# Native fp32 for the last two dense products of self-attention, with one copy of the sums and a new order of the last head group

## The reference

```python
def _L0_attn_ref(x, w_q, w_kv, w_dense):          # HEADS 16, GROUPS 4, KVC 128
    q = einsum('bsh,he->bse', x, w_q).reshape(b, sq, GROUPS, HPG, KVC)
    k, v = split(einsum('bsh,he->bse', x, w_kv), 2, axis=-1)
    scores = einsum('bqgpd,bkgd->bgqpk', q, k) * SCALE
    scores = where(causal, scores, -inf)
    probs = softmax(scores, axis=-1)
    ctx = einsum('bgqpk,bkgd->bqgpd', probs, v).reshape(b, sq, HEADS * KVC)
    return einsum('bse,eh->bsh', ctx, w_dense)
...
x = x + _L0_xattn_ref(_layernorm(x), ctx_1024, ...)
x = x + _L0_attn_ref(_layernorm(x), w_q, w_kv, w_dense)
x = x + _L0_ffn_ref(_layernorm(x), gate_w, ...)   # scores = sigmoid(x @ gate_w), top 2, experts
```

## Time and profile before

| | |
|---|---|
| median of three runs | 351.37 us |
| profiled execution | 349.24 us |
| its span, first to last instruction | 347.5 us |
| PE busy | 331.4 us (95%) |
| DVE, POOL, ACT busy | 271.0, 236.1, 232.4 us |
| chain of waits, PE's share | 71% |

### The profile page before, as it was taken

The page is one execution under the profiler, slowest core; times in us unless marked ns, Lnnn a source line. Parts: engine busy times, 40 slices in busy tenths (PEclk is TensorE's granted clock), DMA queues, the critical chain, the costliest instruction groups (busy, mean ns, idle before and its releaser), DMA issues.

```text
span 347.5 us, 6872 instructions
## 1 busy us (share of the span) xinstructions
PE 331.4 (95%) x2246; PEld 299.8 (86%) x2246; DVE 271.0 (78%) x469; ACT 232.4 (67%) x415; POOL 236.1 (68%) x146
## 2 busy tenths in 40 slices
PE   6899989999999999999999998999899999999995
PEld 5788868898999999999999987999798897698995
DVE  3787788897988988989889887754559745579997
ACT  3789467667687687777767775975355686266761
POOL 4593728798599599499598596859626768507650
PEclk9999999999999999999999999999999999999999
DMA  6811468776886895895795887890232040404630
GB/s 199 249 32 38 100 153 189 196 176 152 220 189 144 204 204 127 208 208 125 178 204 117 201 181 183 208 321 31 87 101 83 2 151 1 144 9 124 179 107 31
DMA packets 32566, 49.98 MB, mean 144 GB/s; under 512 B 5537, under 2 KB 23073, under 8 KB 32545
## 3 DMA queue, kind: packets, MB, share of 16 engines
q1 hardware_dynamic: 32544, 49.72, 56.6%
HBM read 20.08 MB, written 0.26 MB: 59 GB/s over the span
## 4 chain that ended last, share of the span: by engine, by line
PE 71%; DVE 9%; POOL 6%; issue 4%; ACT 4%; SPq 3%; DMA 2%; DVEq 0%; POOLq 0%; ACTq 0%
PE bank L573 10%; PE pair L573 10%; PE bank L574 10%; PE bank L575 10%; PE pair L574 10%; PE pair L575 10%; POOL pT L431 4%; SPq L272 3%; PE bank L717 2%; PE bank L876 1%; DMA ctx_raw<-in_ctx_dram 1%; DVE ctx_raw L1495 1%; PE bank L709 1%; PE pair L869 1%; DMA pT<-blocks 1%
## 5 line engine op out<-in xcount | busy, mean ns | idle before, releaser
L431 POOL TENSOR_TENSOR pT<-pT,pT_hi 128x1024 fp32r<-128x1024 f32 x56 | 133.4, 2407 | 35.3 <-ACT pT_hi L1135 35.3
L1125 ACT ACTIVATE probs<-probs,lowest 128x2048 f32<-128x2048 f32 x32 | 64.3, 2009 | 26.5 <-DVE lowest L1484 26.4
L1135 ACT ACTIVATE pT_hi<-pT 128x1024 fp32r<-128x1024 f32 x56 | 57.6, 1053 | 16.1 <-DMA pT<-ctx_raw 10.5
L573 PE MATMUL bank<-pT_hi,ctx_lo 128*128 128x256 f32 x224 | 63.8, 285 | 0.4 <-POOL pT L431 0.4
L574 PE MATMUL bank<-pT,ctx_hi 128*128 128x256 f32 x224 | 64.1, 286 | 0.0
L575 PE MATMUL bank<-pT_hi,ctx_hi 128*128 128x256 f32 x224 | 63.6, 284 | 0.0
L573 PE MATMUL pair<-ctxT_hi,qk_lo 128*128 128x512 f32 x128 | 52.1, 407 | 2.4 <-DVE lowest L1484 2.0
L575 PE MATMUL pair<-ctxT_hi,qk_hi 128*128 128x512 f32 x128 | 50.1, 391 | 0.0
L574 PE MATMUL pair<-ctxT_lo,qk_hi 128*128 128x512 f32 x128 | 50.1, 391 | 0.0
L1484 DVE CUSTOM_DVE_ANT_0 probs<-pair,mask_bias,lowest 128x1024 f32<-128x1024 f32 x32 | 41.0, 1281 | 9.3 <-PE pair L575 8.5
L431 POOL TENSOR_TENSOR ctx_lo<-ctx_raw,ctx_hi 128x512 fp32r<-128x512 f32 (+1 forms) x19 | 31.5, 1671 | 21.8 <-DVE route L1817 9.4
(11 more groups left out here) (253 smaller groups left out, 841.3 us busy)
## 6 DMA issues: line engine op xcount, KB each, us to landing
pT<-blocks SPq DMA_DIRECT2D x112, 128.0 KB, 2.3
pT<-ctx_raw SPq DMA_DIRECT2D x112, 128.0 KB, 2.3
ctx_raw<-ffn_experts_gate_up_dram SPq DMA_DIRECT2D x16, 256.0 KB, 2.8
wq<-in_L_xattn_Wq_dram SPq DMA_DIRECT2D x8, 256.0 KB, 2.6
ctx_raw<-in_ctx_dram SPq DMA_DIRECT2D x8, 256.0 KB, 6.4
wo<-in_L_xattn_Wo_dram SPq DMA_DIRECT2D x8, 256.0 KB, 2.8
blocks<-in_L_attn_w_dense_dram SPq DMA_DIRECT2D x4, 512.0 KB, 4.6
ctx_raw<-_L_ffn_experts_down_dram SPq DMA_DIRECT2D x16, 128.0 KB, 2.4
```

Of the source, the lines that this page charges most:

```text
L431: pool.tensor_tensor(dst, src, hi.bitcast(F32), ALU.subtract).then_inc(ready, 1)
L573: pe.matmul(dst, w[1], x[0], start=start, stop=False)
L1125: act.activation(probs[:, j], probs[:, j], ACT.Exp, bias=lowest[:, p, j, 1:2], scale=-1.0, accum_out=den[:, p, j:j + 1]).then_inc(exps, 1)
L1135: act.activation(hi_slot(c), chunk(p, c).bitcast(F32), ACT.Copy).then_inc(pT_hi_ready, 1)
```

## The change

- `dense_end` of the last two groups multiplies whole fp32 sums by whole fp32 weights in native matmuls, four for each group and batch, in place of twelve split ones. The sums have one copy each (`c2_whole`, in a buffer that the experts use later), with no rounding and no remainder.
- The rounding of these two groups' weights (DVE, ACT) and POOL's two subtractions are gone.
- The copy of group 2's sums is made by ACT for batch 0, ahead of its last exponentials, and by DVE for batch 1; both copies of group 3's are ACT's.
- DVE normalises the last group's probabilities in place of POOL.
- PE's order in the last group is new, and the eight `keep_warm` in it are gone; between the two transposes of the normed rows there is one `keep_warm` in place of two.
- ACT copies each batch's normed rows whole and then rounded; DVE subtracts from the whole copy in SBUF. PE waits for the remainders behind the logits, ahead of the first gate product.

```diff
@@ -178,6 +178,7 @@
         sg = ctx_raw[:, 3072:3584].rearrange("p (s t) -> p s t", s=2)
         hT = ctx_raw[:, 3584:4096].rearrange("p (s t) -> p s t", s=2)
+        c2_whole = ctx_raw[:, 3072:4096].rearrange("p (b n) -> p b n", b=B)
@@ -243,7 +244,8 @@
             sem("out_psum"), sem("added"))
         ld_wq2, ld_wkv2, ld_wd2 = [sem(f"ld_wq2_{i}") for i in range(2)], sem("ld_wkv2"), sem("ld_wd2")
-        ld_wd2_last, wd2_last_hi_ready = sem("ld_wd2_last"), sem("wd2_last_hi_ready")
+        ld_wd2_last = sem("ld_wd2_last")
+        c2_whole_ready = [sem(f"c2_whole_ready{b}") for b in range(B)]
         wq2_hi_ready, wk2_hi_ready, wd2_hi_ready = sem("wq2_hi_ready"), sem("wk2_hi_ready"), sem("wd2_hi_ready")
@@ -504,12 +506,8 @@
             def split_d(r):
-                if isinstance(r, int) and r == R - 1:
-                    pool.wait_ge(wd2_last_hi_ready, 1)
-                    rest(wq2_lo, wq2, wq2_hi, wd2_ready)
-                else:
-                    pool.wait_ge(wd2_hi_ready, r + 1)
-                    rest(wd2_lo, wd2, wd2_hi, wd2_ready)
+                pool.wait_ge(wd2_hi_ready, r + 1)
+                rest(wd2_lo, wd2, wd2_hi, wd2_ready)
@@ -541,9 +539,6 @@
             split_expert(0, 0)
             split_expert(0, 1)
-            split_d(R - 2)
-            split_d(R - 1)
-            normalise(R - 1)
             split_expert(0, 2)
@@ -890,14 +885,18 @@
             def dense_end(r, b):
-                hi, lo = (wq2_hi, wq2_lo) if r == R - 1 else (wd2_hi, wd2_lo)
-                pe.wait_ge(wd2_ready, r + 1)
-                pe.wait_ge(c2_ready, 2 * r + b + 1)
+                if r == R - 1:
+                    w = wq2
+                    pe.wait_ge(ld_wd2_last, 16)
+                else:
+                    w = wd2
+                    pe.wait_ge(ld_wd2, 16 * (R - 1))
+                    pe.wait_ge(added2, R - 2)
+                pe.wait_ge(c2_whole_ready[b], r - (R - 2) + 1)
                 for h in range(HR):
-                    cols = slice(h * P, (h + 1) * P)
-                    mm = product(D_LAST[b][:, b * H:(b + 1) * H], (c2_hi[:, b, cols], c2_lo[:, b, cols]),
-                                 (hi[:, h * H:(h + 1) * H], lo[:, h * H:(h + 1) * H]),
-                                 r == R - 2 and h == 0, r == R - 1 and h == HR - 1)
+                    mm = pe.matmul(D_LAST[b][:, b * H:(b + 1) * H], c2_whole[:, b, h * P:(h + 1) * P],
+                                   w[:, h * H:(h + 1) * H],
+                                   start=(r == R - 2 and h == 0), stop=(r == R - 1 and h == HR - 1))
                 if r == R - 1:
@@ -932,19 +931,16 @@
                 for b in range(B):
                     scores2(R - 1, b)
+                    attend2(R - 2, b)
+                dense_end(R - 2, 0)
+                turn2(R - 1, 0)
+                dense_end(R - 2, 1)
+                pe.wait_ge(v2_ready, R)
+                turn2(R - 1, 1)
                 for b in range(B):
-                    attend2(R - 2, b)
-                keep_warm(QB, 8)
-                turn2(R - 1, 0)
-                dense_end(R - 2, 0)
-                attend2(R - 1, 0)
-                turn2(R - 1, 1)
-                dense_end(R - 2, 1)
-                attend2(R - 1, 1)
+                    attend2(R - 1, b)
                 for b in range(B):
                     dense_end(R - 1, b)
-
-
@@ -989,10 +985,10 @@
-            for b in range(B):
-                xn_transpose(b, 2, (bank[2], bank[5])[b])
-                keep_warm(QA, 2)
-            pe.wait_ge(xnT_ready, 3 * B)
+            xn_transpose(0, 2, bank[2])
+            keep_warm(QA, 1)
+            xn_transpose(1, 2, bank[5])
+            keep_warm(QA, 2)
@@ -1028,6 +1024,7 @@
                                    start=(k == 0), stop=(k == HB - 1))
             mm.then_inc(logits, 1)
+            pe.wait_ge(xnT_ready, 3 * B)
             gate_up(0, 0)
@@ -1303,6 +1300,21 @@
                 act.activation(c2_hi[:, b], PC[b][:], ACT.Copy).then_inc(c2_hi_ready, 1)
+            def whole_c(r, b):
+
+                act.wait_ge(c2_psum, 2 * r + b + 1)
+                act.activation(c2_whole[:, b], PC[b][:], ACT.Copy).then_inc(c2_whole_ready[b], 1)
+
+            def last_group2():
+                whole_c(R - 2, 0)
+                for b in range(B):
+                    exps2(R - 1, b)
+                for b in range(B):
+                    act.wait_ge(p2T_psum, 2 * (R - 1) + b + 1)
+                    act.activation(p2T[:, b], TURN2_LAST[b][:], ACT.Copy).then_inc(p2T_ready, 1)
+                for b in range(B):
+                    whole_c(R - 1, b)
+
             def group2(r, before, behind):
@@ -1321,19 +1333,12 @@
                         act.wait_ge(ld_dn[s], 16)
                         act.activation(dn_hi[:, s], ring_dn[:, s], ACT.Copy).then_inc(dn_hi_ready, 1)
-
-                    act.wait_ge(qb_psum, R - 1)
-                    act.wait_ge(ld_wd2_last, 16)
-                    act.activation(wq2_hi, wq2, ACT.Copy).then_inc(wd2_last_hi_ready, 1)
                 if behind:
...
                     act.wait_ge(p2T_psum, 2 * r + b + 1)
-                    src = TURN2_LAST[b] if r == R - 1 else PC[b]
-                    act.activation(p2T[:, b], src[:], ACT.Copy).then_inc(p2T_ready, 1)
-                    if r == R - 1:
-                        copy_c(r, b)
+                    act.activation(p2T[:, b], PC[b][:], ACT.Copy).then_inc(p2T_ready, 1)
@@ -1354,7 +1359,7 @@
             for r in range(1, R - 1):
                 group2(r, True, True)
-            group2(R - 1, True, False)
+            last_group2()
@@ -1363,9 +1368,11 @@
                 act.activation(sg[:, s % 2], GU[s % 2][:, 0:B * T], ACT.Silu).then_inc(silu_ready, 1)
-            rows = [xnT_copy(b, 2, (bank[2], bank[5])[b]) for b in range(B)]
             for b in range(B):
-                xnT_copy_whole(b, 2, rows[b])
+                act.wait_ge(xnT_psum, 2 * B + b + 1)
+                rows = (bank[2], bank[5])[b][:, 0:HB * P].rearrange("p (k t) -> p k t", k=HB)
+                act.activation(xnT[:, :, b * T:(b + 1) * T], rows, ACT.Copy).then_inc(xnT_whole, 1)
+                act.activation(xnT_hi[:, :, b * T:(b + 1) * T], rows, ACT.Copy).then_inc(xnT_hi_ready, 1)
             act.wait_ge(logits, 1)
@@ -1719,7 +1726,7 @@
                 dve.tensor_tensor(rows, D_BANK[:], rows, ALU.add).then_inc(added2, 1)
-            def group2(r, before, behind, split):
+            def group2(r, before, split):
                 for b in range(0 if before else 1, B):
@@ -1730,22 +1737,38 @@
                 if split:
                     round_q(r + 2)
-                if before and behind:
+                if before:
                     add2(r - 1)
-                if behind:
-                    copy_qb(r + 1)
+                copy_qb(r + 1)
                 if split:
                     round_kv(r + 2)
-                if before and behind:
+                if before and split:
                     round_d(r)
+
+            def normalise_last(b):
+                dve.wait_ge(s2_rden, 2 * (R - 1) + b + 1)
+                dve.tensor_tensor(p2[:, b], p2[:, b], rd2[:, b].unsqueeze(2).broadcast_to([P, HR, P]),
+                                  ALU.mult).then_inc(s2_probs, 1)
+
+            def last_group2():
+                for b in range(B):
+                    scale2(R - 1, b)
+                    max2(R - 1, b)
+                invert(R - 1, 0)
+                normalise_last(0)
+                dve.wait_ge(c2_psum, 2 * (R - 1))
+                dve.tensor_copy(c2_whole[:, 1], PC[1][:]).then_inc(c2_whole_ready[1], 1)
+                copy_v(R - 1)
+                invert(R - 1, 1)
+                normalise_last(1)
             round_kv(1)
             first_qb(1, qb_psum, 1, qb_ready)
-            group2(0, False, True, True)
+            group2(0, False, True)
             for r in range(1, R - 2):
-                group2(r, True, True, True)
-            group2(R - 2, True, True, False)
-            group2(R - 1, True, False, False)
+                group2(r, True, True)
+            group2(R - 2, True, False)
+            last_group2()
@@ -1758,13 +1781,19 @@
                 norm_stats(b, 2)
-            rest_c(R - 1)
+            def xnT_rest_whole(b):
+                dve.wait_ge(xnT_whole, B + b + 1)
+                dve.wait_ge(xnT_hi_ready, 2 * B + b + 1)
+                cols = slice(b * T, (b + 1) * T)
+                dve.tensor_tensor(xnT_lo[:, :, cols], xnT[:, :, cols], xnT_hi[:, :, cols].bitcast(F32),
+                                  ALU.subtract).then_inc(xnT_ready, 1)
+
             finish_rows(0)
...
                 norm_apply(b, 2)
             for b in range(B):
-                xnT_rest(b, 2, (bank[2], bank[5])[b])
+                xnT_rest_whole(b)
```

## The result

In the same set of executions the kernel before took 351.15 us (median of 7, 349.68 to 351.54) and the changed one 348.79 (median of 7, 348.04 to 349.98); the ratio is 0.9939, 95% interval 0.9921 to 0.9957. A second set, with 12 and 29 executions, gave 349.09 against 350.21, ratio 0.9961 (0.9933 to 0.9988). The profiled execution of the changed kernel took 348.99 us, with a span of 347.1: only 0.25 less than the profiled execution before. The page shows one reason why this is so little: in one of the forty slices TensorE's granted clock was not full, while it was full throughout in the earlier trace rows.

The account below looks back on a forecast made before the run. Bound by a chain of PE alone up to about 289.5, then hand-overs among PE, ACT, DVE and POOL. Dense end 1.15 + entry 0.70 = 1.85 off 349.24 gives 347.39; plus 2.13 to the median, 349.5 us, range 348.8 to 350.6.

Parts of the forecast that it names:

- Dense calls (a): Last two groups' dense products: four native matmuls take 1.73 us a call against 1.43 split, adding 1.20 us of PE work.
- the rival with 1.90: Dense products: a native matmul costs four split ones, so 1.90 us a call, gain 1.15, end 350.2; chance 0.06.
- Order (b): PE's last head group: reordered steps without fillers end at 299.16 against 300.45, a gain of 1.29 us without waits.
- Waits (c): PE's hand-overs in the last group: 0.15 us charged for waits (none to 0.5), leaving 1.15 at the dense end.
- the 1.1 to 1.3 that the prediction had named as its sign: End of the dense products: DVE's last addition was to come 1.1 to 1.3 us earlier.
- Normalisation on DVE: Last group's probabilities: DVE normalises in 0.69 us, bounds 0.6 and 1.05, in place of POOL's 1.05.
- the rival that has it wait behind POOL: Last group: DVE's normalisation waits up to 1.27 us for a POOL piece, PE loses 1.1, end 350.6; chance 0.09.
- What goes away at no cost (d): Dropped roundings and POOL's subtractions cost nothing now; first down-projection reload moves from 297.88 to about 289, costed at nothing.
- The rival with a larger gain: Layer norm's stretch: reloads leave it and POOL is idle beside DVE, up to 0.7 us more, 348.8; chance 0.09.
- Entry (e): Feed-forward entry: whole rows copied first, so logits, exponential and router come 0.70 us earlier; gate products' wait costs 0.03.
- The rival that gives it back after the router: From 311.7, a fixed event at the expert splits sets the pace; 0.70 is lost, end 350.2; chance 0.12.
- its slower rival: After the dense end: TensorE's clock drops to 1.2 GHz, about 3.2 us more, end 352.7; chance 0.04.

Follow-up runs that it names:

- the run with the dense half alone: Kernel before plus the change's native dense products, new last-group order and DVE normalisation, with the old feed-forward entry; 349.59 us, ratio 0.9986.
- the undisturbed profile: Changed kernel, unaltered, profiled again, with no clock fall ahead of the gate products; end 59.87 us after the last head group's first scores (-1.67).

## Why the prediction was right, step by step

- **Dense calls (a).** Forecast 1.73, measured 1.73 (289.67 to 291.40, 296.15 to 297.88), as in the earlier trace rows, and the same in every run with native products where nothing held them. That is 1.21 times the 1.43 of the split form, and the rival with 1.90 fell. The Trainium skill, "FP8 and Floating Point Precision", section TensorE Precision Notes, has four passes for true fp32; the estimate of 1.91 drawn from it took a pass to be as long as a split matmul (0.119). The measured time doesn't speak against four passes, only against that: by them a pass would be 1.73/16 = 0.108 us, an estimate, as no row shows single passes.
- **Order (b).** Forecast 1.29 without waits. The new order has every step where it was put, and the run with the old order shows that this step carries the gain: 2.09 lie between the two (about 1.7 without ACT's share in it), against 1.20 that the slower products cost.
- **Waits (c): the term that was mis-sized.** Charged 0.15 with bounds of none to 0.5; measured 0.42: from the start of the first native product to the end of the last one PE took 297.88 + 1.89 - 289.67 = 10.10, where the prediction had 9.52 and a tail of 0.16. The second product waited 0.20 for DVE's copy, which began at 291.21 and ended at 291.89, and ran 0.07 longer for it (1.96 against 1.89). The four sums were stretched by 0.16, from 1.88 to 2.04: ACT's copy of the second turned block ended at 294.48 + 0.60 = 295.08, in time for a sum at 294.28 + 0.86 = 295.14, but PE's weight load stands behind the same wait, and that came only at 295.19. The row of weight loads (start, us, line, operation, shape, count, idle time before) shows it:

```profile
292.01 1.59 PEld L897 LDWEIGHTS pair<-blocks,ctx_raw 128*128 128x128 f32 x8 [0.24 <-issue]
...
295.19 0.30 PEld L871 LDWEIGHTS bank<-probs 128*128 128x128 f32 x2 [0.72 <-issue]
```

At both places the load starts 0.11 to 0.12 behind the end of the copy that it waits for; the prediction counted 0.03 for a hop, read from a POOL step to a turn and from ACT to DVE. The first cause was shown by taking the copy away from DVE (0.26); the second is read from the trace only. So the dense end gave 0.89 and not 1.15, and stayed under the 1.1 to 1.3 that the prediction had named as its sign.
- **Normalisation on DVE.** Forecast 0.69 between 0.6 and 1.05; measured 0.69. POOL was through with its splits at 287.55 + 2.51 = 290.06 and DVE began at 290.60, so the rival that has it wait behind POOL did not come up; its margin was 0.54.
- **What goes away at no cost (d).** The first reload of a down projection was issued at 289.00 (forecast about 289; the earlier trace rows has 297.88). From the addition to the exponential the kernel before takes 5.02, and the run with the dense half alone 5.01 though these reloads have left that stretch (DMA share 0.00 to 0.04 from 298 to 306): they cost nothing that a mark shows. The rival with a larger gain, which rested on them, fell with that.
- **Entry (e).** Forecast 0.70; measured 0.74 in the run that has this part alone, and 1.63 - 0.89 = 0.74 in the whole change. The rival that gives it back after the router fell: in the undisturbed profile the end has 1.67 of it all. At the silu, though, 0.19 to 0.20 of it is missing (-0.54 alone, -1.44 in the whole): there PE's gate products, which now wait for the remainders, decide and not the exponential, as the 0.20 of idle time ahead of the silu shows. The prediction had put this wait at 0.03. At the end it is back.
- **The sum.** Forecast -1.85, measured -1.67 from S to the end without a fall: 0.26 less at the dense end, 0.04 more at the entry.
- **The clock.** The prediction put its slower rival at 3.2 us, by the transposes, logits and first gate products together. A fall did come there, in one profile of the change out of two, later than thought and shorter: the transposes and logits were through at full clock, it began at about 304.1, and it cost 1.06. What the prediction held against it, no hole on PE before 299 and five fillers behind, did not prevent it. The place was right and the price three times too high. Executions with a mean granted clock of 0.995 or less are about as frequent before and after (55 of 78, 13 of 19), so the falls did not turn the sign.
- **Carrying the sum over to the median: in part luck.** The step "profiled execution plus 2.13" took the 2.13 for a fixed distance. It is made by the executions with a fall: the first profile of before had none. Profiles without a fall ahead of PE's last matmul took 349.24, 349.55 and 349.25 before and 347.96 after, 1.28 to 1.59 less. The measured 348.79 lies not in the forecast's own 349.1 to 350.0 but at the lower edge of the whole range, though the gain from S on was smaller than forecast. The medians differ by 351.15 - 348.79 = 2.36 because they stand for different levels: the 351.15 is near the 351.40 that executions of before with a mean clock of 0.99 or less have (the clocks of those seven are not known), and the middle one by clock of the seven changed ones has 0.995. One level is worth 351.40 - 350.24 = 1.16, which leaves 1.2 for the change. The second set gave 350.21 - 349.09 = 1.12. So the step gave a time within range, but was no reason. The 0.1 to 0.4 between the profiles' 1.28 to 1.59 and the 1.67 from S on lies mostly ahead of S, where PE's list is the same (S at 285.96, 286.30 and 286.00 before, 286.33 after without a fall); what moves it stayed open.

## What to carry to other kernels

A slower instruction can win where it takes steps out of a hand-over and lets the order fill the wait with work; price the order and the instruction separately, since here the one was worth 1.7 to 2.1 us and the other cost 1.20. When such an order leaves only tenths of cover, list each copy with its engine and the moment it is wanted: the copy charged at 0.1 was the longest wait, and another engine had room for it. Before a profiled difference is believed or carried over to a median, read the granted clock of both executions, compare marks on both sides of a fall, and compare executions of like mean clock.

## What the runs showed of the hardware

TensorE's granted clock fell to 1.2 GHz for 3 to 4 us in some executions of one and the same program and not in others. Where PE still had work it was seen at three places (53 to 58, 218 to 222 and 304 to 310 us), each behind a stretch with PE idle for part of the time; but PE was busy 2.02 of the 4 us from 50 to 54 in the profile of the kernel before that fell and 2.04 in the three that didn't, and the two profiles without fillers had the same gaps ahead of the gate products and differed all the same. What decides it was not found. Ahead of the gate products a fall cost 0.87 and 1.06 us at the end. In the undisturbed profile of the change the clock also fell at 345 us, behind PE's last matmul (342.15), where it costs nothing: its mean of 0.998 is still one without a fall that counts, while the kernel before has 1.000 in its profiles without a fall.

Grouped by the mean granted clock, 78 executions of the kernel before had medians of 349.48 (23, above 0.9975), 350.24 (28, 0.993 to 0.995) and 351.40 (27, 0.99 or less); 19 of the changed kernel had 348.15 (6), 348.99 (9) and 350.32 (4). Level by level the change is worth 1.1 to 1.3 us over all sets (1.0 to 1.5 in the second set alone, which ran side by side on one chip), and each further step down costs 0.8 to 1.3: as much as the change itself.
